# Transposing DMAs for the odd tiles of the first layer of a three-layer graph network with a gated feed-forward block

## What is computed

```python
def gnn(x, src, dst, W_self, W_neigh, b):
    deg = maximum(segment_sum(ones, dst), 1)
    h = x
    for l in range(3):
        h_neigh = segment_sum(h[src], dst) / deg
        h = relu(h @ W_self[l] + h_neigh @ W_neigh[l] + b[l])
        h = h / maximum(norm(h), 1e-12)
    return h
x = x + gnn(layernorm(x), src, dst, ...)
x = x + ffn(layernorm(x), ...)   # 8 experts, the best 2 of each row, then a layernorm
```

## Time and profile before

| | us |
|---|---|
| median of three runs | 2080.27 (2074.16 to 2082.3) |
| the profiled execution, its own time | 2078.15 |
| its span, first to last instruction | 2076.4 |
| first layer on PE, tile 0 to the start of tile 78 | 24.3 to 487.9 |
| first gather of the second layer issued | 494.48 |

### The profile page before, as it was taken

How to read it: one execution, slowest core, us unless ns; L and a number is a source line. 1 busy time by engine, 2 the same in 40 slices (tenths; PEclk the granted TensorE clock), 3 DMA queues, 4 the chain that set the end, 5 groups by cost and what they waited for, 6 DMA issues and landing times.

```text
span 2076.4 us, 41132 instructions
## 1 busy us (share of the span) xinstructions
PE 1957.9 (94%) x13965; PEld 1064.1 (51%) x13965; DVE 1627.2 (78%) x3951; ACT 1034.4 (50%) x1877; POOL 1225.1 (59%) x1239
## 2 busy tenths in 40 slices
PE   6999999997999999999999999999899999999996
PEld 2444444443444444444444444444467767677774
DVE  7677986665777777776777777775689999999985
ACT  4444333332334434343344444553677777777762
POOL 2785116674656665664444444454568888888854
PEclk9999999998999999999999999999999999999998
DMA  6877678974787878874788886555878888878863
GB/s 209 205 184 230 238 253 151 142 136 119 189 192 202 193 196 188 202 187 147 207 236 233 235 233 191 175 172 165 224 171 180 183 186 186 182 179 181 185 99 50
DMA packets 330680, 384.93 MB, mean 185 GB/s; under 512 B 200057, under 2 KB 200231, under 8 KB 330471
## 3 DMA queue, kind: packets, MB, share of 16 engines
q1 hardware_dynamic: 269655, 216.86, 43.1%
q0 software_dynamic: 60816, 165.43, 31.1%
HBM read 175.81 MB, written 165.31 MB: 164 GB/s over the span
## 4 chain that ended last, share of the span: by engine, by line
PE 41%; DVE 25%; issue 12%; ACT 9%; DMA 8%; POOL 4%; SPq 0%; DVEq 0%; ACTq 0%; POOLq 0%
PE psY L578 18%; PE psS L578 18%; DMA w_n<-HH 6%; DVE R L1485 4%; ACT RR L1013 2%; POOL node_info L769 2%; DVE w_s L1693 2%; DVE area L1473 2%; DVE HH L1509 2%; DVE area L1683 2%; DVE st6b L1670 2%; PE psT L1798 2%; DVE w_s L1658 2%; DVE HH L1590 2%; DVE G L1473 1%
## 5 line engine op out<-in xcount | busy, mean ns | idle before, releaser
L578 PE MATMUL psY<-w_n,HT 128*128 128x512 f16 x1620 | 378.8, 384 | 21.8 <-DVE HT L1357 12.7
L578 PE MATMUL psS<-w_s,HT 128*128 128x512 f16 x1620 | 371.7, 379 | 0.0
L1013 ACT ACTIVATE RR<-R 128x512 f32<-128x512 f32 x237 | 149.6, 631 | 312.8 <-DVE R L1485 312.7
L878 POOL DMA_INDIRECT y_rows<-YB,poutT x158 | 160.8, 1018 | 198.0 <-DVE YB L1364 161.6
L578 PEld LDWEIGHTS psY<-w_n,HT 128*128 128x128 f16 x1620 | 157.5, 99 | 224.5 <-DVE HT L1357 23.9
L578 PEld LDWEIGHTS psS<-w_s,HT 128*128 128x128 f16 x1620 | 154.4, 98 | 167.8
L1374 DVE SCALAR_TENSOR_TENSOR SB<-psS,downs,bias 128x512 f32<-128x512 f32 x237 | 177.6, 749 | 76.6 <-PE psS L578 74.5
L578 PE MATMUL psY<-w_n 128*128 128x512 f16 x960 | 220.5, 379 | 12.4 <-DMA w_n<-HH 12.2
L578 PE MATMUL psS<-w_s,w_n 128*128 128x512 f16 x960 | 220.3, 379 | 0.0
L578 PE MATMUL psS<-w_w,w_s 128*128 128x512 f16 x948 | 217.5, 379 | 0.8 <-ACT w_s L1108 0.8
L1364 DVE SCALAR_TENSOR_TENSOR YB<-psY,YB 128x512 f16<-128x512 f32 x237 | 162.4, 685 | 47.8 <-ACT YB L980 47.6
(11 more groups left out here) (328 smaller groups left out, 3895.9 us busy)
## 6 DMA issues: line engine op xcount, KB each, us to landing
self_rows<-SB SPq DMA_DIRECT2D x236, 256.0 KB, 2.5
Sl<-self_rows SPq DMA_DIRECT2D x158, 256.0 KB
area<-in_x_dram SPq DMA_DIRECT2D x78, 256.0 KB, 5.1
y_rows<-YB SPq DMA_DIRECT2D x78, 256.0 KB, 5.1
out_dram<-obb SPq DMA_DIRECT2D x78, 256.0 KB
raw<-in_L_gnn_W_neigh_dram SPq DMA_DIRECT2D x12, 256.0 KB, 3.6
raw<-in_L_gnn_W_self_dram SPq DMA_DIRECT2D x12, 256.0 KB, 4.2
y_rows<-YB,poutT POOLq DMA_INDIRECT x158
```

Source lines behind the costliest of these rows:

```text
L578: mm = eng.matmul(acc, lhs[:, a, c, :], w[:, bpart, c, :], start=(c == 0 and n == 0), stop=(stop and c == KC - 1 and n == 2))
L878: pool.indirect_dma_start(Yd[l][:, :], bass.IndirectOffsetOnAxis(ap=poutT[:, t.t:t.t + 1], axis=0), YB[i][:, :], None, bounds_check=node_l ...
L1013: act.activation(RR[i][:, :], R[i][:, :], ACT.Relu).then_inc(s.rr, 1)
```

## The change

From tile 5 on the odd tiles of the first layer (5, 7, ... 77: 37 tiles) are no longer turned by PE and copied by ACT. SP issues a transposing DMA of the tile's HH instead, in step s for tile s+2, as the last stage of the step: behind `load_x` of s+5 and `store` of s-1, ahead of the step's stores of `out_dram` and of the next step's `load_x`. It waits for `hhi` and `hlo` of its tile and, by ring, for `own` of the tile eight back. The turned rows go into a ring of four buffers, `HTD0`, in `area` (the large scratch that also holds the x ring). `neigh` waits for the landing (`hd`) instead of for ACT's copy; `hi0` of tile t waits for the landing of tile t-2's DMA where that one was turned so. All even tiles from 4 on now share psT0 and HT0, so PE's `turn` waits for the copy of the tile turned before.

```diff
+N_DMA0 = 5
+def by_dma0(t):
+    return t.t % 2 == 1 and t.t >= N_DMA0
+        HTD0 = [as_turned(area[:, 8 * D + D * i:8 * D + D * (i + 1)]) for i in range(HD_RING)]
...
+            def turn_rows0(t):
+                if not by_dma0(t):
+                    return
+                i = t.slot(2)
+                sp.wait_ge(s.hhi, (t + 1).n)
+                sp.wait_ge(s.hlo, (t + 1).n)
+                after(sp, s.sp, (t + (1 - 2 * HD_RING)).n)
+                sp.dma_start_transpose(turned_rows(t, 0).rearrange("p a c n -> p (a c) n"),
+                                       HH[i].rearrange("p a n -> p (a n)")).then_inc(s.hd[dma_slot0(t)], 16)
-            run_plan(TN, [(5, load_x), (-1, store)],
+            run_plan(TN, [(5, load_x), (-1, store), (2, turn_rows0)],
...
             def hi0(t):
                 act.wait_ge(s.rr, (t + 1).n)
-                after(act, s.tr, (t + -1).n)
+                if t.t >= 2 and by_dma0(t + -2):
+                    act.wait_ge(s.hd[dma_slot0(t + -2)], dma_landed0(t + -2))
+                elif t.t >= 2:
+                    act.wait_ge(s.tr, turned_by_pe(t + -2, 0))
...
             def turn0(t):
+                if by_dma0(t):
+                    return
...
             def turn(t, l):
+                if l == 0 and by_dma0(t):
+                    return
-                    after(pe, s.ht, early_turned(t, l) - (2 if l == 0 else 1))
+                    after(pe, s.ht, early_turned(t, l) - (2 if l == 0 and t.t < N_DMA0 else 1))
...
             def neigh(t, l):
-                if by_dma(t, l):
+                if l == 0 and by_dma0(t):
+                    pe.wait_ge(s.hd[dma_slot0(t)], dma_landed0(t))
+                elif by_dma(t, l):
```

More of the change, by code:

```diff
@@ L159, in by_dma, with turned_by_dma0 @@
     return (l == 1 and t.t % 2 == 1 or l == 2 and t.t >= 2) and t.t < late_from(l)
+def by_dma0(t):
+    return t.t % 2 == 1 and t.t >= N_DMA0
+def turned_by_dma0(t):
+    return len([k for k in range(t.t + 1) if by_dma0(Tile(k))])
 def dma_tile(n):
@@ L174, in turned_by_pe @@
 def turned_by_pe(t, l):
-    return t.n + 1 - (turned_by_dma(t) if l else 0)
+    return t.n + 1 - (turned_by_dma(t) if l else turned_by_dma0(t))
 def late_turned(t, l):
@@ L209, in __init__ @@
         self.ht = sem("p0_ht")
+        self.hd = [sem(f"p0_hd{i}") for i in range(HD_RING)]
         self.y = sem("p0_y")
@@ L513, in build, with as_turned, dma_slot0, dma_landed0 @@
         HTD = HTR[0:HD_RING]
+        def as_turned(words):
+            return words.bitcast(F16).rearrange("p (a c n) -> p a c n", a=2, c=KC)
+        HTD0 = [as_turned(area[:, 8 * D + D * i:8 * D + D * (i + 1)]) for i in range(HD_RING)]
+        def dma_slot0(t):
+            return (turned_by_dma0(t) - 1) % HD_RING
+        def dma_landed0(t):
+            return 16 * ((turned_by_dma0(t) - 1) // HD_RING + 1)
         def dma_slot(t):
@@ L519, in dma_landed @@
             return 16 * ((turned_by_dma(t) - 1) // HD_RING + 1)
-        def as_turned(words):
-            return words.bitcast(F16).rearrange("p (a c n) -> p a c n", a=2, c=KC)
         HT_LATE = [as_turned(area[:, 8 * D + D * i:8 * D + D * (i + 1)]) for i in range(LATE[1])]
@@ L528, in turned_rows @@
             k = late_place(t, l)
+            if l == 0 and by_dma0(t):
+                return HTD0[dma_slot0(t)]
             if by_dma(t, l):
@@ L982, in turn0 @@
             def turn0(t):
+                if by_dma0(t):
+                    return
                 i = t.slot(2)
-                act.wait_ge(s.tr, (t + 1).n)
+                act.wait_ge(s.tr, turned_by_pe(t, 0))
                 after(act, s.sp, (t + -1).n)
```

## The result

| | before | after |
|---|---|---|
| median | 2075.29 us (9 runs, 2072.74 to 2084.23) | 2085.71 us (9 runs, 2081.84 to 2100.05) |
| the profiled execution, its own time | 2078.15 | 2087.05 |
| its span | 2076.4 | 2085.3 |
| mean granted clock of PE | 0.991 | 0.989 |

The ratio is 1.0053, with an interval of 1.0036 to 1.0070: the change costs about 10 us. The forecast was 2089 us in a range of 2074 to 2109.

A forecast was written before the change was run, and what follows sets the result against it. POOL's scatters were taken to bound the first layer up to 184 us and from 323 us, DVE and PE between. +2 - 2.7 + 9.2 = +8.5 us on 2078.15 gave 2086.7; from the three-run median 2080.27, 2089 us, range 2074 to 2109.

The forecast's parts named there:

- early term: node_info scatters, 53 to 184 us: added DMAs lengthen POOL's short waits, +2 us within bounds of 0 and 5.7.
- scatter term: slot_table scatters, 323 to 460 us: half of each DMA's 0.80 us a step slows POOL, 0.40 x 23 groups = +9.2 us.
- gain in steps 36 to 47: Up to 307 us, where PE sets the pace: six turns of 0.45 us fall away, -2.7 us.
- The end, 0: Step 78 to the first gather: POOL's table, not PE, is late by 0.73 us, so no gain or loss, 0.
- From step 48 on PE runs into POOL's pace, 0: Steps from 48 on: PE loses 14 or 15 turns, 6.5 us, but POOL's pace limits it, so 0 gained.
- A: Rival, chance 0.26: the added DMAs are absorbed, scatters and loads land as before, the -2.7 us gain stays; 2077 us.
- C: Rival, chance 0.06: PE was the bound after all, the whole 16.7 us of removed turns is gained; 2063.6 us.
- B: Rival, chance 0.23: the new DMA's landing sets PE's two-step pace from 8.9 us on; 2104.6 us at an 11 us landing.

The follow-up runs named there:

- e11: The change for tiles 5 to 27 alone (12 DMAs), all other tiles turned by PE as in the kernel before; ratio 1.0006.
- e4: The change for tiles 37 to 47 alone (six), all other tiles turned by PE as in the kernel before; 2082.92 us, ratio 1.0036.
- e9: The changed kernel once more, unedited, beside the kernel before on a third chip; 2086.85 us, ratio 1.0039.
- e3: The changed kernel with the transposing DMA moved behind the next load of x and ahead of the store of y; 2094.75 us, ratio 1.0091.
- e6: The kernel before with only SP's new waits for hhi and hlo and no DMA behind them, on the slower chip; ratio 0.9998.
- e5: The kernel before once more, unchanged, on the slower chip; 2085.18 us.
- e12: The change for tiles 49 to 77 alone (15 DMAs), all other tiles turned by PE as in the kernel before; ratio 1.0028.
- e1: The changed kernel with odd tiles from 5 on turned by nobody, no DMA, their products reading a constant buffer; 2078.18 us, ratio 1.0002.
- e2: The kernel before with the 37 transposing DMAs added into an unused ring, PE and ACT still turning all tiles; 2086.56 us, ratio 1.0047.
- e10: The kernel before with the transposing DMAs added into an unused ring and nothing removed, run again on a third chip; ratio 1.0043.
- e8: The kernel before with two transposing DMAs added for each odd tile, into two unused rings, on the slower chip; 2111.98 us, ratio 1.0145.
- e7: The kernel before with 37 plain copies of the same bytes added into an unused ring, on the slower chip; ratio 1.0010.

## Why the prediction was right

**The sum.** Forecast +8.5 us on the profiled execution, 2086.7; measured 2087.05. The first `slot_table` scatter was to stay near 322.66 and is at 323.02, the first gather was to leave at about 503 and leaves at 503.28, with nothing changed behind it. By the medians the change costs 10.4 us in both comparisons, by the ratios 11.0 and 8.1. The absolute forecast came out 3.3 us high because I added it to a median of three runs, 2080.27; with nine runs that median is 2075.29, 5 us lower. That base was the larger mistake, and it hid that the change itself costs a little more than the sum. That 8.5 and the 8.80 of the first gather agree so well is in part luck: of the 8.80, 1.19 us arose before the first new DMA, what was measured of the early term is about 1 us less than forecast, of the scatter term 2 to 3 us less, of the gain in steps 36 to 47 0.9 us less, and at the end there is a loss that the forecast put at nothing. On POOL's list 2.47 us of it stand between group 23 and the table load, 1.9 of them in the last landing (a wait of 6.16 us against 4.28): I had the landings recover when the load of x ends, at about 460 us, but from 460 to 480 us the DMA share is now 0.77 where it was 0.40.

**Early, +2 us.** Size and place are right at tile 24, but most of it doesn't last. All six profiles with transposing DMAs there, one for an odd tile, have 121.75 to 123.56 us from tile 5 to 24; the four without on the same chips 119.17 to 120.41. Until tile 36 part is given back: 70.73 to 71.21 us against 71.57 to 75.87. From tile 5 to 36 after is 0.95 us behind before, e11 1.15. Tile 24 to 36 is DVE's, and DVE catches up what it owes because its small work there isn't tied to PE's tiles; that last reason is only argued. At the end e11's first gather is 0.5 us later than before's, so what failed is that the whole delay under the first scatters is passed on. e11's time, 1.0006, can't settle it: its interval is -1.7 to +4.2 us and holds the +2.

**Steps 36 to 47, -2.7 us.** The sign is right by the profiles: -1.79 in after, -2.80 in e4, -4.35 and -4.36 in e9 and e3. The last two are more than six turns can give, and e6 has -1.61 against e5 with all its turns, so part of these numbers is not the turns'.

**Scatter stretch, +9.2 us.** The mechanism was right: DMAs that add time on the engines (1.60 us by the forecast, 1.7 to 2.6 by the rises of the share), the later landings, the waits for `slot_table` over 20.1 us and groups over 6.01. The size was somewhat high. I had 0.40 us a group; measured were 0.28 and 0.24 in after, 0.35 and 0.29 with the DMAs only added, 0.42 in e12. For the 23 groups that is 6.35 us in after, where the forecast had 9.2. By PE's tiles 48 to 78 it is +7.2 and +5.2 us. That the time on the 16 engines is the part of the DMA that hurts, and not its thousand packets or its hold on SP, is argued and not shown. Half of the added engine time was a guess in the middle of 0 and all; it is 0.3 to 0.5 of it.

**The end, 0.** Wrong by 1.29 us. I knew that the table comes last and took its delay as part of the scatters' term. I had not seen that PE then pauses, that the clock falls, and that the matmuls on which the first gather waits pay for it. The same extra stands in e9 (8.15 us) and e12 (8.23); in e1, e2, e4, e10 and e11 it is 6.53 or 6.54.

**From step 48 on PE runs into POOL's pace, 0.** Nearly right. In before, 30 tiles take 168.94 us, exactly 30 times PE's 5.63: PE does set the tiles' pace there. But POOL is close behind. With the turns gone (e1) it is 167.16 us and not 162.2. So 1.78 of 6.7 us were there to gain, and the DMAs took them.

**Rivals.** A (absorbed, 2077) falls by the ratios of after, e9, e2 and e10. C (PE the bound, 2063.6) falls by e1: even without any DMA the median doesn't move beyond its interval, and the first layer gets 6.2 us shorter, not 16.7. B needed a landing of over 8.9 us; the median was 7.5, near the 7.3 us of x in before, and PE's two steps take 11.7 us in the mean, over the 10.6 of 3.1 plus the landing. That doesn't mean that the landing ended no waits: six of eleven odd tiles start right behind it, mostly because the DMA leaves late, when HH has waited for DVE and DVE for POOL. Against B speak e2 and e10, where PE waits for none of them, ACT for two (5.6 us) and one (3.2 us), and the loss is the same. e8 shows B's mechanism at twice the load, and e3 with the DMA behind the load of x. The guess that the landing is nearer 9 than 12 us erred on the high side: it is that of x.

**What stays open.** e4's 6.7 us: six DMAs away from all scatters cost more in the median than nothing, its first layer is no longer than before's by more than 0.3 us, and its profile has the excess in the second layer, where the kernel is the same. The three parts (e4, e11, e12) sum to 14.5 us by their ratios, the whole to 8 to 11. The stretch behind the first gather varies over 1578.2 to 1590.2 us between the profiles, 1582.0 and 1590.2 for the same kernel after; all but 0.8 us of it arises before the third layer. In three of the five slower ones PE waits longer for the second layer's own transposing DMAs: 20.3 us in e4, 17.6 in e3 and 17.2 in e9 over the 400 us from 40 us behind the first gather, 13.1 in after; in e1 and e2 it is 13.7 and 13.3. What sets that off was not found. It doesn't carry the verdict on the change, which rests on the times, but it means that a difference of 5 us in one profile can't be put down to one edit.

## What to carry to other kernels

Moving work from a busy engine to DMA is only free if the DMA engines have room where it runs: read their share, stretch by stretch, and price the new DMA by the time that its like takes of the 16 engines, not by bytes alone. Before removing work from the busiest engine, run the kernel with that work left out altogether: here it showed that turning these rows elsewhere could bring some 6 us in the first layer, and nothing that the median shows. And hold medians against each other only from the same chip; take the base from more than three runs.

## What the runs showed of the hardware

- A transposing DMA of 256 KB brings about a thousand packets under 512 bytes. Four of them alone took 1.60 us of all 16 engines each, a plain 256 KB 0.75 us. One held SP for 1.23 us at the median, a plain copy of e7 for 0.47. The plain copies of the same bytes cost the kernel some 2 us for 37, with an interval from -0.8 to 5.2, the transposing ones 9 to 10 on other chips. The Trainium skill, "Advanced Engine Details and Errata", section X-Bar Transpose (TRN2), has them as fast as regular ones; the measurement decides, and it says otherwise.
- The busy share of the DMA engines can read over 1 (1.09, 1.12, 1.16 in e8): the packets' times overlap, so it is no longer occupancy.
- A pause of PE of 3.04 us in the middle of the kernel was followed by a granted clock of 0.70 over the next 5 us, and twelve matmuls in 4.04 instead of 2.75 us. After and e1 have a mean clock of 0.989 at the median of their runs, before 0.991 to 0.992; e12, where PE does less too, has 0.992.
- The kernel before takes 2076 us on two chips and 2085 on a third, all with the same clock (0.991 to 0.992 at the median); in the one profile of each the difference shows in the scatter stretch (6.24 against 6.01 us a group).
